# SyncE's order of key stores, context loads and first-unit loads in a four-layer Flamingo block

## The chip, the cores and the metric

The kernel runs on one core of one Trainium2 chip. The metric is device time in microseconds (us) of one execution, lower is better. Before the change three executions took 1684.19, 1691.92 and 1699.02 us; the median is 1691.92 us.

## The reference

Four layers follow one another on x (4 batches x 256 tokens x 128 features). Each is a gated cross-attention of 16 heads of 8 features over a context of 1601 tokens a batch, and then a gated feed-forward part; every layer projects its own keys and values from the same context.

```
x = x + jnp.tanh(g_xattn[0]) * _L0_xattn_ref(_layernorm(x, axis=-1), ctx_1024, ctx_1024, ctxb_2048x8, ...)
x = x + jnp.tanh(g_ffn[0]) * _L0_ffn_ref(_layernorm(x, axis=-1), L0_ffn_W_fc, ...)
x = x + jnp.tanh(g_xattn[1]) * _L1_xattn_ref(_layernorm(x, axis=-1), ctx_1024, L1_xattn_q_w, ...)
x = x + jnp.tanh(g_ffn[1]) * _L1_ffn_ref(_layernorm(x, axis=-1), L1_ffn_Wr, ...)
x = x + jnp.tanh(g_xattn[2]) * _L2_xattn_ref(_layernorm(x, axis=-1), ctx_1024, L2_xattn_wq, ...)
x = x + jnp.tanh(g_ffn[2]) * _L2_ffn_ref(_layernorm(x, axis=-1), L2_ffn_w_freq_real, ...)
x = x + jnp.tanh(g_xattn[3]) * _L3_xattn_ref(_layernorm(x, axis=-1), ctx_1024, ctx_1024, mask_1x1xSxS2_bk1, ...)
x = x + jnp.tanh(g_ffn[3]) * _L3_ffn_ref(_layernorm(x, axis=-1), L3_ffn_gate_w, ...)
```

An attention is, with h heads and `scale = Dh ** (-0.5)`:

```
scores = jnp.einsum('bhqd,bhkd->bhqk', Q, K) * scale
attn = jax.nn.softmax(scores, axis=-1)
out = jnp.einsum('bhqk,bhkd->bhqd', attn, V)
return out.transpose(0, 2, 1, 3).reshape(B, T, H * Dh) @ Wo.T
```

The second layer has two attentions, a local one (the 256 tokens against themselves) and a global one (against the context), mixed by a gate. The fourth layer masks scores by a 256 x 1601 mask.

## The kernel before

**Stages.** The context is transposed once, in the first layer, and kept in device memory as `ctxT_d` (one 128 x 1601 f32 matrix, 800 KB, a batch). In each later layer a stage that this text calls the key stage runs over the four batches: SyncE loads `ctxT_d` of a batch into one of two slots of `ctxT`; TensorE projects keys (`score_ring`, four matmul columns of 400) and values (`exp_ring`, `pv_bank`); ScalarE writes the keys' first f16 half into `k1c` (line 824), VectorE the rest into `k2c` (line 1062), each with two slots; values go to `v_all` (ScalarE, line 831, in the third and fourth layer; VectorE, line 1069, in the second). Three DMAs of 400 KB a batch store the key halves in `k_d`, in a layout by units (`k_store`, lines 503 and 505). Then comes the attention itself, over 16 units of one batch and four heads. Queries are stored in `q_d` (`q_store` on SyncE, two parts; the third part by GpSimd at line 720).

**Attention.** For a unit, pass 1 (`kp1`, `qp1`, line 1549, or 1545 with the mask) computes scores only for their row maxima, which VectorE takes (line 1132, or 1125 with the mask); pass 2 (`kp2`, `qp2`) computes them again into `exp_ring` for the exponentials on ScalarE and the products with values. `pass1` and `pass2` each load 400 KB of keys and four 12 KB pieces of queries. TensorE's program puts the whole key stage ahead of the first score: `kv(r)`, then `attention(r)`, which starts with the 16 pieces of unit 0, then `r.ahead` = 9 pieces of unit 1 (one of them a transposition of the maxima), and then merged units.

**Who waits for whom in the key stage.** Batch 2 can be projected when its context has landed in the slot that batch 0 leaves (`c_load` waits for TensorE's batch 0). ScalarE can write batch 2's keys when batch 0's three stores have landed (`k_out[0]`), batch 3's when batch 1's have (`k_out[1]`). The last piece of attention work waits for the copies of batch 3.

**SyncE's order.** SyncE carries out `k_prep` in program order, and a wait of it holds everything behind: contexts 0 and 1, the query stores, context 2, keys of batch 0, context 3, keys of batch 1, then a wait and the loads of the first units (in the second layer the eight loads of 256 KB each for the local attention, `local_loads`, lines 530 and 531), then keys of batches 2 and 3. In the second layer the loads of the first global units (`loads_start`) stand behind all stores and are followed by `local_maxima`, small loads (line 539) that the local attention's second pass (line 1652) waits for; the local first pass is line 1640.

**The mask.** In the fourth layer the mask is transposed on TensorE (`mask_turn`, line 1512, 13 times, eight matmuls each, copied by ScalarE at lines 841 to 846), one turn behind each of the first 13 pieces of unit 0.

## Time and profile before

| | |
|---|---|
| median of three executions | 1691.92 us |
| the profiled execution's own time | 1697.42 us |
| its span, first to last instruction | 1695.7 us |
| TensorE busy | 1508.3 us, 89% |
| VectorE busy | 1305.3 us, 77% |
| ScalarE busy | 1164.5 us, 69% |
| GpSimd busy | 149.2 us, 9% |
| mean granted TensorE clock | 0.915 of 2.4 GHz |
| moved by DMA | 119.39 MB, mean 70 GB/s |

Key stages stand at about 398 to 426 us (second layer), 902 to 930 us (third) and 1232 to 1260 us (fourth). A row of the timeline is: start, duration, engine, line, operation, what it writes and reads, how many, and in brackets the idle time ahead of it on its engine and what ended it. SPq rows are SyncE issuing DMAs: their duration is the issue, not the transfer. A granted clock of 1.00 is 2.4 GHz, 0.50 is 1.2 GHz.

### The profile page before, as it was taken

Reading aid. Unit: us, or ns where it says so; the run is one execution under the profiler, and the core shown is the slowest. Engines: PE = TensorE matmul, PEld = TensorE weight load, DVE = VectorE, ACT = ScalarE, POOL = GpSimd, SP = SyncE. Lnnn points to the kernel's source line nnn. Section 1 sums busy time; section 2 is a strip of 40 time slices with the busy share of each in tenths; the row PEclk is TensorE's granted clock in tenths of the full one; section 3 lists DMA queues with packets and bytes.
Section 4 is the critical chain, followed back from the end, with each engine's and each line's share of the span. In section 5 each row is a group of like instructions: output and inputs, shape, how many; then the busy total and the mean of one; then the engine's idle time right before and its main releaser. Section 6 shows DMA issues by size and latency. Waiting matters only on the chain.

```text
span 1695.7 us, 45795 instructions
## 1 busy us (share of the span) xinstructions
PE 1508.3 (89%) x15521; PEld 657.7 (39%) x15521; DVE 1305.3 (77%) x2224; ACT 1164.5 (69%) x2209; POOL 149.2 (9%) x246
## 2 busy tenths in 40 slices
PE   6789999978689999995997799999788999999977
PEld 4423333346233333334674233332453444434355
DVE  5789999546778999944875999997447888888258
ACT  3269999843357899982984499998354777777636
POOL 4200000012000000002221000000100000000012
PEclk9789999989588999996998799999787999999969
DMA  8932122105311221210116221121061111111001
GB/s 205 308 109 65 56 65 56 61 1 167 98 34 45 56 64 54 65 37 13 51 52 188 62 66 55 54 65 52 22 207 45 46 43 45 53 43 44 15 18 33
DMA packets 85286, 119.39 MB, mean 70 GB/s; under 512 B 18967, under 2 KB 57390, under 8 KB 85198
## 3 DMA queue, kind: packets, MB, share of 16 engines
q1 hardware_dynamic: 81694, 109.05, 22.1%
q0 software_dynamic: 2560, 8.20, 1.6%
q8 instruction: 59, 0.97, 0.2%
q10 hardware_dynamic: 944, 0.93, 0.2%
q14 instruction: 29, 0.24, 0.0%
HBM read 83.48 MB, written 34.49 MB: 70 GB/s over the span
## 4 chain that ended last, share of the span: by engine, by line
PE 66%; DVE 16%; issue 8%; ACT 3%; DMA 2%; SPq 2%; POOL 1%; DVEq 0%; ACTq 0%; POOLq 0%
PE pv_bank L1587 21%; DVE mx L1132 11%; PE exp_ring L1575 10%; PE score_ring L1549 5%; PE exp_ring L1567 4%; PE score_ring L1545 4%; PE score_ring L1815 4%; PE exp_ring L1826 3%; PE exp_ring L1572 3%; PE score_ring L1470 2%; PE exp_ring L1477 2%; DMA k_d<-k2c 2%; PE pv_bank L1663 1%; PE score_ring L1728 1%; ACT early L876 1%
## 5 line engine op out<-in xcount | busy, mean ns | idle before, releaser
L876 ACT ACTIVATE early<-exp_ring 128x512 f32<-128x512 f32 (+1 forms) x1664 | 884.3, 599 | 233.8 <-PE exp_ring L1575 115.6
L1132 DVE TENSOR_REDUCE mx<-score_ring 128x2 f32<-128x802 f32 (+1 forms) x768 | 703.2, 984 | 36.4 <-PE score_ring L1549 36.4
L1587 PE MATMUL pv_bank<-early,vg 128*32 128x256 f32 x6656 | 528.5, 396 | 0.7 <-issue 0.2
L1549 PE MATMUL score_ring<-kp,qp 64*128 64x401 f16 (+1 forms) x1536 | 310.8, 350 | 36.0 <-DVE mx L1132 32.0
L1575 PE MATMUL exp_ring<-qp,kp 64*128 64x512 f16 (+1 forms) x1248 | 313.6, 390 | 16.1 <-DMA qp<-ms 11.7
L1587 PEld LDWEIGHTS pv_bank<-early,vg 128*32 128x32 f32 x6656 | 139.1, 108 | 239.5 <-issue 117.1
L1575 PEld LDWEIGHTS exp_ring<-qp,kp 64*128 64x128 f16 (+1 forms) x1248 | 95.3, 95 | 194.7 <-ACT early L876 152.0
L1549 PEld LDWEIGHTS score_ring<-kp,qp 64*128 64x128 f16 x1536 | 76.2, 93 | 194.8 <-DVE mx L1132 169.1
L1545 PE MATMUL score_ring<-kp,qp 64*64 64x400 f16 (+1 forms) x1024 | 137.3, 355 | 11.3 <-DVE mx L1125 9.1
L1567 PE MATMUL exp_ring<-qp,kp 64*64 64x512 f16 x832 | 129.8, 399 | 2.8 <-DMA qp<-ms 2.8
L1572 PE MATMUL exp_ring<-ctxT,mask_eye 64*64 64x512 f16 x800 | 126.1, 385 | 0.0
L698 POOL COPY vg<-v_all 128x416 f32 (+1 forms) x48 | 25.4, 533 | 813.3 <-PE pv_bank L1587 760.6
L942 ACT ACTIVATE early<-score_ring,b_now 128x512 f32<-128x512 f32 x96 | 67.6, 704 | 23.0 <-PE score_ring L1815 22.9
L1312 DVE TENSOR_TENSOR v_all<-early,v_all 128x512 f16<-128x512 f32 x96 | 64.7, 695 | 24.1 <-ACT v_all L944 23.5
L1125 DVE CUSTOM_DVE_ANT_1 wprT<-score_ring,mask_add 128x800 f16<-128x800 f32 x64 | 63.7, 996 | 21.9 <-PE score_ring L1545 19.4
L1062 DVE SCALAR_TENSOR_TENSOR k2c<-score_ring,cols,k1c 128x401 f16<-128x401 f32 (+1 forms) x64 | 38.3, 634 | 54.6 <-ACT k1c L824 53.9
L1125 DVE CUSTOM_DVE_ANT_0 wfcT<-score_ring,mask_add 128x802 f16<-128x802 f32 x64 | 63.5, 992 | 15.9 <-PE score_ring L1545 14.5
L1125 DVE CUSTOM_DVE_ANT_0 wprT<-score_ring,mask_add 128x802 f16<-128x802 f32 x64 | 63.5, 992 | 14.6 <-PE score_ring L1545 12.4
L1182 DVE TENSOR_SCALAR rec<-score_ring 128x16 f32<-128x16 f32 x32 | 5.6, 174 | 88.6 <-PE score_ring L1728 88.6
L1826 PE MATMUL exp_ring<-v_all 128*128 128x128 f16 x1152 | 69.7, 219 | 3.0 <-DVE v_all L1312 2.8
L1567 PEld LDWEIGHTS exp_ring<-qp,kp 64*64 64x64 f16 x832 | 42.2, 105 | 77.0 <-issue 69.6
L1826 PEld LDWEIGHTS exp_ring<-v_all 128*128 128x128 f16 x1152 | 66.4, 98 | 12.4 <-issue 7.0
(271 smaller groups left out, 1504.1 us busy)
## 6 DMA issues: line engine op xcount, KB each, us to landing
kp<-k_d SPq DMA_DIRECT2D x128, 400.2 KB
k_d<-k1c SPq DMA_DIRECT2D x32, 400.2 KB, 6.9
ctxT<-ctxT_d SPq DMA_DIRECT2D x12, 800.5 KB, 5.8
qp<-q_d SPq DMA_DIRECT2D x512, 12.0 KB
k_d<-k2c SPq DMA_DIRECT2D x16, 400.2 KB, 7.9
k_d<-v_loc POOLq DMA_DIRECT2D x12, 400.2 KB, 11.1
ctxT_d<-ctxT SPq DMA_DIRECT2D x4, 800.5 KB, 7.0
o_all<-in_ctx SPq DMA_DIRECT2D x4, 768.0 KB
```

Source lines behind the costliest of these rows:

```text
L876: act.activation(pt[g][0:rows_, 2 * h:2 * h + 2, :], bank[0:rows_, :].rearrange("p (i q) -> p i q", q=S), ACT.Exp).then_inc(exped, 1)
L942: act.activation(hT[hf][:, c, :], PB[(hf * cc + c) % 4], func, bias=b1_now[k][:, c:c + 1], scale=1.0 / WSCALE)
L1125: dve.tensor_tensor_reduce(out=masked[j % 2][:, :, 0:w], in0=src, in1=mask_add[:, qt, c:c + 2, 0:w], scale=1.0, scalar=-3.0e38, op0=ALU.ad ...
L1132: dve.tensor_reduce(dst, src, AX.X, ALU.max).then_inc(score_free, 1)
L1545: ins = pe.matmul(pa[slot][u:u + 2 * R, z, 0:w], qp1[par][rows_, i, qt * P + u:qt * P + u + 2 * R], kp1[par][rows_, at:at + w], start=True ...
L1549: ins = pe.matmul(pa[slot][:, z, 0:w], qp1[par][rows_, i, qt * P:qt * P + P], kp1[par][rows_, at:at + w], start=True, stop=True)
L1567: pe.matmul(bank[out_, :], kp2[par][half, at:at + 2 * R], qp2[par][half, 2 * h:2 * h + 2, :], start=True, stop=False)
L1572: ins = pe.matmul(bank[out_, :].rearrange("p (i q) -> p i q", q=S), mask_eye[half, half], hide.unsqueeze(1).broadcast_to([2 * R, 2, S]), s ...
L1575: ins = pe.matmul(bank[0:rows_, :], kp2[par][half, s * P:s * P + rows_], qp2[par][half, 2 * h:2 * h + 2, :], start=True, stop=True)
L1587: ins = pe.matmul(po[R * j:R * j + R, 0:S], vg[par][0:rows_, s, j, :], pt[g][0:rows_, j, :], start=(s == 0), stop=(s == r.kt - 1))
L1815: ins = pe.matmul(PB[(hf * cc + c) % 4], wus[k][wp][:, c * P:c * P + P], xs[xp][:, hf * 512:hf * 512 + 512], start=(i == 0), stop=(i == 2))
L1826: ins = pe.matmul(PB[4 + hf][:, T * D:T * D + D], hs[hf][hp][:, c, T * P:T * P + P], wds[k][wp][:, c * D:c * D + D], start=(c == 0 and i = ...
```

## The change

SyncE's `k_prep` is split into one for the first layer, `k_prep_first`, with the same order as before, and one for the later layers with another order. In the third and fourth layer: keys of batch 0, context 2, the wait for the landed keys of batch 0 and the query stores, pass 1 loads of units 0 and 1, keys of batch 1, context 3, pass 2 load of unit 0, keys of batches 2 and 3. In the second layer: the waits for the query and local key stores and the eight local loads, then keys of batch 0, context 2, keys of batch 1, context 3, keys of batches 2 and 3, and then the local maxima of batch 0 ahead of the wait for all key stores. In TensorE's program the 13 mask turns of the fourth layer move from between the pieces of unit 0 to ahead of the pieces of unit 1, two a piece. `aside` is always false in the new code, so the lines under it are not built; `kv_key` and `kv_value` emit what `kv` emitted.

```
+            def k_prep(r):
+                g, l = r.ctx, r.layer
+                for i in range(2):
+                    sp.wait_ge(ctx_out[i], 16 * B // 2)
+                c_load(r, g, 0)
+                c_load(r, g, 1)
+                q_store(l)
+                if l == 1:
+                    sp.wait_ge(q_out, 16 * Q_DMAS[l])
+                    sp.wait_ge(q_out2, 16 * l * Q2_DMAS)
+                    sp.wait_ge(padded, 16 * B * (len(RUNS) - 1))
+                    sp.wait_ge(lk_out, 16 * LK_DMAS)
+                    local_loads()
+                k_store(r, g, 0)
+                c_load(r, g, 2)
+                if l > 1:
+                    sp.wait_ge(q_out, 16 * Q_DMAS[l])
+                    sp.wait_ge(q_out2, 16 * l * Q2_DMAS)
+                    sp.wait_ge(k_out[0], 48 * (B // 2 * g + 1))
+                    pass1(r, 0, 0)
+                    pass1(r, 1, 1)
+                k_store(r, g, 1)
+                c_load(r, g, 3)
+                if l > 1:
+                    sp.wait_ge(fill, r.fill0)
+                    pass2(r, 0, 0)
+                k_store(r, g, 2)
+                k_store(r, g, 3)
+                if l == 1:
+                    local_maxima([0])
...
-            def loads_start(r):
+            def loads_behind_local(r):
                 pass1(r, 0, 0)
                 pass1(r, 1, 1)
-                if r.layer == 1:
-                    local_maxima()
-                    sp.wait_ge(fill, RUNS[LOCAL].fill0 + HG * HG)
-                elif r.u0:
-                    sp.wait_ge(fill, r.fill0)
+                local_maxima(range(1, B))
+                sp.wait_ge(fill, RUNS[LOCAL].fill0 + HG * HG)
                 pass2(r, 0, 0)
...
                     for k, j in r.pieces(first=True):
                         piece(0, 0, k, first=True)
-                        if r.mask and j < KT:
-                            mask_turn(j)
                 for k in range(r.ahead):
+                    if r.mask:
+                        for m in range(2 * k, min(2 * k + 2, KT)):
+                            mask_turn(m)
                     piece(1, 1, k)
```

How the order moves on SyncE in the third layer, behind the query stores (the fourth layer reads alike). Here `ctxT<-ctxT_d` is a context load, `k_d3<-k1c` and `k_d3<-k2c` are key stores, `kp1_0`, `kp1_1` and `qp1_0`, `qp1_1` are pass 1 loads of units 0 and 1. Before:

```order
L497 DMA ctxT<-ctxT_d 128x1601 [waits v_ps,k_ps]
L503 DMA k_d3<-k1c 16x8x1601 [waits k_1]
L503 DMA k_d3<-k1c 16x8x1601
L505 DMA k_d3<-k2c 16x8x1601 [waits k_2]
L497 DMA ctxT<-ctxT_d 128x1601 [waits v_ps,k_ps]
L503 DMA k_d3<-k1c 16x8x1601 [waits k_1]
L503 DMA k_d3<-k1c 16x8x1601
L505 DMA k_d3<-k2c 16x8x1601 [waits k_2]
L515 DMA kp1_0<-k_d3 128x1601 [waits k_out_0,q_out2,q_out]
L517 DMA qp1_0<-q_d2 24x256 x4
L515 DMA kp1_1<-k_d3 128x1601
L517 DMA qp1_1<-q_d2 24x256 x4
```

And after the change:

```order
L520 DMA k_d3<-k1c 16x8x1601 [waits k_1]
L520 DMA k_d3<-k1c 16x8x1601
L522 DMA k_d3<-k2c 16x8x1601 [waits k_2]
L514 DMA ctxT<-ctxT_d 128x1601 [waits v_ps,k_ps]
L532 DMA kp1_0<-k_d3 128x1601 [waits k_out_0,q_out2,q_out]
L534 DMA qp1_0<-q_d2 24x256 x4
L532 DMA kp1_1<-k_d3 128x1601
L534 DMA qp1_1<-q_d2 24x256 x4
L520 DMA k_d3<-k1c 16x8x1601 [waits k_1]
L520 DMA k_d3<-k1c 16x8x1601
L522 DMA k_d3<-k2c 16x8x1601 [waits k_2]
L514 DMA ctxT<-ctxT_d 128x1601 [waits v_ps,k_ps]
```

Batch 0's stores now come ahead of context 2, and the wait for `k_out_0` with the four rows of pass 1 loads now stands ahead of batch 1's stores and context 3, which it stood behind.

On SyncE in the second layer, behind the query stores (`w_up`, `w_dn`, `kp2`, `wfcT` and `wprT` are the places that the local queries and keys are loaded into). Before:

```order
L497 DMA ctxT<-ctxT_d 128x1601 [waits v_ps,k_ps]
L503 DMA k_d2<-k1c 16x8x1601 [waits k_1]
L503 DMA k_d2<-k1c 16x8x1601
L505 DMA k_d2<-k2c 16x8x1601 [waits k_2]
L497 DMA ctxT<-ctxT_d 128x1601 [waits v_ps,k_ps]
L503 DMA k_d2<-k1c 16x8x1601 [waits k_1]
L503 DMA k_d2<-k1c 16x8x1601
L505 DMA k_d2<-k2c 16x8x1601 [waits k_2]
L530 DMA w_up_0<-q_d1 128x4x256 [waits lk_out,padded,zeroed,q_out2,q_out]
L531 DMA kp2_0<-k_d1 128x4x256
L530 DMA w_up_1<-q_d1 128x4x256
L531 DMA kp2_1<-k_d1 128x4x256
```

And after the change:

```order
L547 DMA w_up_0<-q_d1 128x4x256 [waits lk_out,padded,zeroed,q_out2,q_out]
L548 DMA kp2_0<-k_d1 128x4x256
L547 DMA w_up_1<-q_d1 128x4x256
L548 DMA kp2_1<-k_d1 128x4x256
L547 DMA w_dn_0<-q_d1 128x4x256
L548 DMA wfcT<-k_d1 128x4x256
L547 DMA w_dn_1<-q_d1 128x4x256
L548 DMA wprT<-k_d1 128x4x256
L520 DMA k_d2<-k1c 16x8x1601 [waits k_1]
L520 DMA k_d2<-k1c 16x8x1601
L522 DMA k_d2<-k2c 16x8x1601 [waits k_2]
L514 DMA ctxT<-ctxT_d 128x1601 [waits v_ps,k_ps]
```

The eight local loads and their wait moved from behind batch 1's stores to ahead of batch 0's, and both context loads went with the stores to behind them.

On TensorE in the fourth layer, where unit 0's scores start (`kp1_0` is unit 0, `kp1_1` unit 1, `mask01` the mask). Before, at the start of unit 0:

```order
L1545 MATMUL score_ring_0<-kp1_0,qp1_0 64x401 [waits in1_0,score_free,k_2,v_ok]
L1545 MATMUL score_ring_0<-kp1_0,qp1_0 64x401 x3
L1512 MATMUL exp_ring_0<-ident16,mask01 64x128 x8
L1545 MATMUL score_ring_1<-kp1_0,qp1_0 64x401 [waits score_free]
L1545 MATMUL score_ring_1<-kp1_0,qp1_0 64x401 x3
L1512 MATMUL exp_ring_1<-ident16,mask01 64x128 x8
L1545 MATMUL score_ring_0<-kp1_0,qp1_0 64x401 [waits score_free]
L1545 MATMUL score_ring_0<-kp1_0,qp1_0 64x401 x3
L1512 MATMUL exp_ring_2<-ident16,mask01 64x128 x8
L1545 MATMUL score_ring_1<-kp1_0,qp1_0 64x401 [waits score_free]
```

And after the change, where unit 1 starts:

```order
L1573 MATMUL score_ring_1<-kp1_0,qp1_0 64x400 [waits score_free]
L1573 MATMUL score_ring_1<-kp1_0,qp1_0 64x400 x3
L1540 MATMUL exp_ring_0<-ident16,mask01 64x128 x8
L1540 MATMUL exp_ring_1<-ident16,mask01 64x128 x8
L1573 MATMUL score_ring_0<-kp1_1,qp1_1 64x401 [waits score_free,in1_1]
L1573 MATMUL score_ring_0<-kp1_1,qp1_1 64x401 x3
L1540 MATMUL exp_ring_2<-ident16,mask01 64x128 x8
L1540 MATMUL exp_ring_0<-ident16,mask01 64x128 [waits mt_ok]
L1540 MATMUL exp_ring_0<-ident16,mask01 64x128 x7
L1573 MATMUL score_ring_1<-kp1_1,qp1_1 64x401 [waits score_free]
L1573 MATMUL score_ring_1<-kp1_1,qp1_1 64x401 x3
```

Unit 0's pieces have no turn between them any more, and unit 1's first six pieces have two each, the seventh one.

## Rows read from the trace of the kernel before

**Rows 1.** Page, part 4: chain that ended last, shares by engine.

```profile
PE 66%; DVE 16%; issue 8%; ACT 3%; DMA 2%; SPq 2%; POOL 1%; DVEq 0%; ACTq 0%; POOLq 0%
```

**Rows 2.** Stretch of third layer: busy by engine, granted clock, DMA share, GB/s.

```profile
909.00:935.00 26.00, 19.06 (x113) 13.14 (x112) 11.82 (x18) 11.38 (x24) 1.00 (x2) 0.92 0.99 307
```

**Rows 3.** Chain in order of time, end of that stage: start us, us, what.

```profile
915.96 10.04 DMA k_d<-k2c
...
928.07 1.60 ACT v_all L831 x4
```

**Rows 4.** Timeline of SyncE's DMA issues, same stage.

```profile
903.48 5.17 SPq L512 DMA_DIRECT2D q_d<-q1c  x8
...
908.75 0.53 SPq L497 DMA_DIRECT2D ctxT<-ctxT_d  x1
...
910.55 0.93 SPq L505 DMA_DIRECT2D k_d<-k2c  x1
...
914.02 1.90 SPq L503 DMA_DIRECT2D k_d<-k1c  x2
...
922.26 1.61 SPq L517 DMA_DIRECT2D qp<-q_d  x4
```

**Rows 5.** Timeline of TensorE (PE) and ScalarE (ACT), same stage and its end.

```profile
914.49 2.96 PE L1470 MATMUL score_ring<-ctxT,wsq 128*128 128x401 f32 x8 [0.92 <-DMA ctxT<-ctxT_d]
...
919.06 2.05 ACT L824 ACTIVATE k1c<-score_ring,cols 128x401 f16<-128x401 f32 x4 [4.92 <-DMA k_d<-k2c]
...
920.87 2.96 PE L1470 MATMUL score_ring<-ctxT,wsq 128*128 128x401 f32 x8 [0.52 <-DMA ctxT<-ctxT_d]
...
929.77 0.52 PE L1549 MATMUL score_ring<-kp,qp 64*128 64x401 f16 x4 [3.04 <-ACT v_all L831]
...
931.21 0.52 PE L1549 MATMUL score_ring<-kp,qp 64*128 64x401 f16 x2 [0.92 <-DVE mx L1132]
```

**Rows 6.** Landing: context loads (line 497, all), key stores (505, third layer).

```profile
DMA to landing us min/median/max: 4.4/5.8/8.3
...
DMA to landing us min/median/max: 5.5/7.3/10.0
```

**Rows 7.** Timeline of the fourth layer: SyncE, and TensorE's first score.

```profile
1238.56 0.53 SPq L497 DMA_DIRECT2D ctxT<-ctxT_d  x1
...
1259.56 0.53 PE L1545 MATMUL score_ring<-kp,qp 64*64 64x401 f16 x4 [2.10 <-ACT v_all L831]
```

**Rows 8.** Chain in the fourth layer: a turn and the next piece.

```profile
1263.44 0.58 PE exp_ring L1512 x8
...
1264.02 0.80 PE score_ring L1545 x2
```

**Rows 9.** Timeline of TensorE, same layer, two pieces without turns.

```profile
1281.61 1.80 PE L1545 MATMUL score_ring<-kp,qp 64*64 64x401 f16 x8 [0.45 <-DVE mx L1125]
```

**Rows 10.** Timeline of the second layer: GpSimd's local key stores, TensorE.

```profile
397.51 6.25 POOL L655 DMA_DIRECT2D k_d<-xn  x12
...
410.04 2.96 PE L1470 MATMUL score_ring<-ctxT,wsq 128*128 128x401 f32 x8
...
426.31 0.63 PE L1640 MATMUL score_ring<-kp,w_up 32*128 32x256 f16 x8 [3.50 <-DVE v_all L1069]
...
443.25 0.62 PE L1652 MATMUL exp_ring<-w_up,kp 32*128 32x256 f16 x6 [1.13 <-DMA w_up<-on]
```

**Rows 11.** Landing of line 655; first and last rows of eight local loads.

```profile
DMA to landing us min/median/max: 1.9/2.3/2.5
...
L530 SPq DMA_DIRECT2D w_up<-q_d x2: 653/1790/2928, 412.7 to 414.3; - x2
...
L531 SPq DMA_DIRECT2D wprT<-k_d x1: 793/793/793, 422.6 to 422.6; - x1
```

**Rows 12.** Chain: the four matmuls of line 1486, second layer, then fourth.

```profile
391.06 1.83 PE score_ring L1486 x4
...
1227.71 3.43 PE score_ring L1486 x4
```

More of the change, by code:

```diff
@@ L150 @@
 LOCAL = 1
+Q_DMAS = [12, 20, 28, 36]
+Q2_DMAS, LK_DMAS = 4, 12
 LEAD = 7
@@ new lines, in k_prep_first @@
+            def k_prep_first(r):
+                sp.wait_ge(dconst, 4)
+                constant_rows(r)
+                ctx_load(2)
+                q_store(0)
+                for b in range(B):
+                    sp.wait_ge(ctx_e, 4 * b + 4)
+                    sp.dma_start(ctxT_d[b], ctxT[:, b % 2, :]).then_inc(ctx_out[b % 2], 16)
+                    if b == 0:
+                        ctx_load(3)
+                    k_store(r, 0, b)
+                    if b == 1:
+                        sp.wait_ge(q_out, 16 * 12)
+                        sp.wait_ge(padded0, 16 * B)
+                        sp.wait_ge(dconst, 9)
+                        sp.wait_ge(prep_w, 10)
+                        sp.wait_ge(prep_v, 11)
+                        sp.wait_ge(k_out[0], 48)
+                        pass1(r, 0, 0)
+                        pass1(r, 1, 1)
+                        pass2(r, 0, 0)
@@ L531, in local_loads, with local_maxima @@
                     sp.dma_start(kl[b], k_d[LOCAL][HG * b:HG * b + HG].rearrange("n p q -> p n q")).then_inc(lin[b], 16)
-            def local_maxima():
-                for b in range(B):
+            def local_maxima(batches):
+                for b in batches:
                     sp.wait_ge(lp_free, ROWS_AT[b] + 1)
@@ L821, in k_split @@
                     for c in range(4):
[L822 removed]
+                        lo, n_ = c * w + min(c, 1), w + (c == 0)
+                        bank = PB[4 + c] if aside else PB[c]
                         act.wait_ge(k_ps, 4 * n + c + 1)
[L824 removed]
+                        act.activation(k1c[:, b % 2, lo:lo + n_], bank[:, 0:n_], ACT.Identity,
                                        bias=col(BK[r.index])).then_inc(k_1, 1)
[L827 removed]
+                        if aside:
+                            act.activation(kf[:, 4 * (b - 2) + c, 0:n_], bank[:, 0:n_], ACT.Identity,
+                                           bias=col(BK[r.index])).then_inc(k_f, 1)
+                    for c in range(4 if aside or not BV[r.index] else 0):
                         k = 4 if c < 3 else 1
@@ L1450, in normT, with kv_key, kv_value @@
                         ins.then_inc(ln_t, 1)
+            def kv_key(r, b, c, bank):
+                n, w = B * r.ctx + b, S2 // 4
+                lo = c * w + min(c, 1)
+                pe.matmul(bank[:, 0:w + (c == 0)], sq(WK[r.index]), ctxT[:, b % 2, lo:lo + w + (c == 0)],
+                          start=True, stop=True).then_inc(k_ps, 1)
+            def kv_value(r, b, c):
+                for k in range(4 * c, min(4 * c + 4, KT)):
+                    pr = P if k < FULL else TAIL
+                    ins = pe.matmul(PB[4 + c][0:pr, (k % 4) * VW:(k % 4) * VW + VW],
+                                    ctxT[:, b % 2, k * P:k * P + pr], sq(WV[r.index]), start=True, stop=True)
+                ins.then_inc(v_ps, 1)
             def kv(r):
                 g = r.ctx
-                w = S2 // 4
                 pe.wait_ge(q_f, 2 * (r.layer + 1))
```

70 lines of the change are left out of this document (16 added, 54 removed).

## The prediction

> **What bounds the kernel now.** I read the page first, for who ends the chain: TensorE has 66% of it, VectorE 16%, DMA only 2% and SyncE 2% [rows 1]. So most of the span cannot feel this change; it can act only where TensorE waits for SyncE's queue, and those places are the three key stages. The chain in order of time says what ends the third layer's stage: batch 1's last key store (10.04 us from its issue to its landing), which ScalarE waits for before it may write batch 3's keys, then the value copies [rows 3]. SyncE's timeline gives the order of issues and their lengths [rows 4], TensorE's and ScalarE's the waits: TensorE waits 0.92 and 0.52 us for contexts 2 and 3, ScalarE 4.92 us for batch 0's stores, and the first score follows batch 3's copies after 3.04 us of idling [rows 5]. It does not wait for its own keys. The stretch table shows the DMA engines full for these 26 us: share 0.99, 307 GB/s [rows 2]. The fourth layer's stage is the same picture [rows 7].
>
> TensorE's program is unchanged in this stage: all four batches are projected before the first score. Loading unit 0 earlier therefore starts nothing earlier, while what is put behind those loads (batch 1's stores, context 3) is just what the stage's end hangs on.
>
> **Third layer, step by step.** SyncE ends the query stores at 903.48 + 5.17 = 908.65 [rows 4]. Batch 0's keys were ready by then (before, their three stores were issued without a pause behind context 2), so its three stores now go first; as before they take 2.1 us (1.2 us for two, 0.93 for the third): 910.8. The last of them, issued at 909.9, lands 5.5 to 10.0 us later [rows 6]; with no context ahead of it I take 6.1, near the minimum: 916.0. Context 2 is issued behind them, 910.8 instead of 908.75, lands at about 917, and TensorE does batch 2 until about 923. That isn't on the path. SyncE stands until 916.0, then issues ten loads at 0.40 us each (four took 1.61 [rows 4]) and two gaps: 4.2 us, 920.2. Batch 1's stores take 2.1 to 3.0 us (their first two took 1.90 [rows 4]): 2.4, so 922.6, where before they were out by about 917. Then context 3, formerly issued just ahead of 914.02, lands 4.4 / 5.8 / 8.3 us later [rows 6]; behind 1.2 MB of stores I take 6.2: 928.8. Batch 1's stores land at about the same time, so one wait covers both.
>
> From there TensorE needs its whole batch: batch 2 ran from 914.49 to 920.35 (920.87 less 0.52 idle), 5.9 us [rows 5]. Copies and the first score add 0.5 (four copies took 1.60, and the last is a small one [rows 3]). Sum 935.2.
>
> To this comes the clock. TensorE would idle from about 923 to 928.8. In the trace it was at 2.4 GHz at 929.77 after 3.0 us of idling (four matmuls in 0.52 us) and at 1.2 GHz at 931.21 (two in 0.52) [rows 5]; a six-us hole should end in the low clock. At its start after such a pause a run of four matmuls took 3.43 us where it took 1.83 in the second layer [rows 12], 1.6 us more; batch 3 is longer, so I take 2.0 us. End 937.2 against 929.77: **+7.4 us**. The Trainium skill ("TensorE: Matmul & The Clock Gate", "Part 1: The HAM clock gate") speaks against this change in the same way: the array's full clock is released by sustained activity and withdrawn after idling. By that rule the holes below cost their 2 us each; without it the whole sum would be 6 us less.
>
> Bounds: all short landings and no clock loss give 915.4 + 4.0 + 2.1 + 4.4 + 5.9 + 0.5 = 932.3, +2.5. All long (917.2, then 4.8 for loads issued a sixth slower, 3.0 + 8.3 + 5.9 + 2.8 + 0.5) give 942.5, +12.7.
>
> **Fourth layer.** The same issues begin at 1238.56 instead of 908.75 [rows 4, 7], so the end is 937.2 + 329.8 = 1267.0 against 1259.56 [rows 7]: **+7.5 us**, same bounds.
>
> Mask turns: before, a piece and a turn on TensorE take 0.80 + 0.58 = 1.38 us [rows 8], at the low clock; without a turn two pieces take 1.80 + 0.45 = 2.25, or 1.12 each, set by VectorE [rows 9]. Before: 13 x 1.38 + 12 x 1.12 = 31.4. After: unit 0's 16 pieces at 1.12 = 17.9; five pieces of unit 1 with two turns at 0.80 + 1.16 = 1.96; the maxima's piece with two, 1.5; one with one, 1.38; two at 1.12: 32.8. Bundled in pairs the turns overflow VectorE's shadow by more than singly: **+1.5 us** (0 if the clock is high there, 3 at worst).
>
> **Second layer.** The local loads now wait for GpSimd's local key stores, issued until 397.51 + 6.25 = 403.8 and landed 1.9 to 2.5 us after issue [rows 10, 11]: 405.7. The eight loads were issued from 412.7 to 422.6 + 0.8, 10.7 us with two issues of about 3 us against a full queue; the shortest were 0.65 [rows 11]. They hold 2.1 MB, 6.8 us at 307 GB/s [rows 2]; I take 7.0 for the issue. Context 2 then has 2.1 + 1.2 MB ahead of it: 4.1 MB from about 407.2 on is 13.4 us, landing 421.6, where batch 2 began at 410.04 [rows 10]. Batch 2 takes 5.9 + 2.0 (TensorE idled twelve us): 429.5. Context 3 (6.1 MB, 428.1) is there by then. Batch 3 and copies: 435.9 against 426.31 [rows 10], +9.6. Given back: local maxima of batch 0 go ahead of the global loads, which removes at most the 1.13 us that line 1652 waited for them [rows 10]. **+8.5 us**; bounds +3.1 (issue in 6.0 us, batch 0's stores in 2.1, context 2 landing 4.4 us later at 418.2, two batches of 5.9, 0.5, no clock loss, 1.1 given back) and +13.5 (issues of 10.7 us again, 2.8 us of clock).
>
> **Sum.** 7.4 + 7.5 + 1.5 + 8.5 = 24.9 us. Nothing downstream absorbs it: behind each stage comes attention in which TensorE is busy. The profiled execution took 1697.4 us, 5.5 more than the median of the runs; so 1722.3 in its terms, and 1691.9 + 24.9 = **1716.8 us** against the median.
>
> **Rivals.**
> - *Cheap.* Short landings and a clock that stays up: about 19 (the sum less 6) less 5 of shorter waits, +14, 1706 us. For it: the queues are emptier when SyncE stands. Against: a hole of six us. 0.17.
> - *Dear.* The local loads block the queue as before and the landings are at their medians or above: +34, 1726 us. For it: share 0.99 [rows 2]. Against: fewer transfers overlap. 0.17.
> - *Hidden.* The bytes are the same and the DMA engines full, so each stage ends with the last byte as before: within 3 us, 1692. Against: TensorE waits for particular bytes, and SyncE standing about five us per layer leaves the engines empty. 0.04.
> - *Faster.* Batch 1's stores, whose 10.04 us end the stage [rows 3], no longer share the engines with a context issued ahead (0.8 MB, 2.6 us at 307 GB/s). If they kept their place, three stages end 2.6 us sooner and the local maxima give 1.1: 1683 us. It decides at batch 0's landing: with 4.2 us of loads between, it must land by 914.0 - 4.2 = 909.8, before its last store's issue ends. 0.04.
>
> **How the numbers follow.** The forecast, 1709 to 1725 us, has 0.58. The range 1700 to 1729 takes in the cheap rival and the dear one; its low end is the sum of all low bounds (2.5 + 2.5 + 0 + 3.1 = 8.1), its high end +37, short of all high bounds together (41.9), which need every landing at its maximum. About 1% is what a measurement can tell from no change, here 17 us. Slower by over 1% (above 1708.8): forecast, dear and 0.02 of the cheap one, 0.77. Within 1%: the rest of the cheap one and the hidden one, 0.19. Faster: 0.04.
>
> **What would show it.** In the third and fourth layer SyncE's pass 1 loads are issued at about 916 and 1246 from the old starts, batch 1's stores six us later than before; TensorE waits about 6 us for context 3 where it waited 0.5, and the chain shows that load and batch 3's matmuls at the low clock in place of the 10.04 us store. In the second, TensorE's wait of some 12 us stands ahead of batch 2. Unit 0's masked pieces come every 1.12 us and unit 1's first ones every 2. I am wrong if batch 0's stores land within 4 us, if context 3 overtakes them, or if TensorE does not wait for it.

## The result and the profile after

The changed kernel takes 1730.15 us (median of six executions, 1722.51 to 1732.12) against 1691.07 us (1684.19 to 1699.02, six): a ratio of 1.0215, 95% interval 1.0188 to 1.0242. It is slower by 39 us where 25 were forecast. Its median lies 1.2 us above the high end of the range, 1729 us; reckoned from the 1691.92 us that the prediction started from, the ratio gives 1728.3 us, just inside it. The ratios in this text leave out single executions far above the rest: one of e9 (1763.1 us), one of e11 (2023.6 us) and two of the kernel before (3206.7 and 4334.1 us).

| | before | after |
|---|---|---|
| the profiled execution's own time | 1697.42 us | 1732.12 us |
| its span | 1695.7 us | 1730.4 us |
| TensorE busy | 1508.3 us, 89% | 1525.4 us, 88% |
| VectorE busy | 1305.3 us, 77% | 1307.0 us, 76% |
| ScalarE busy | 1164.5 us, 69% | 1167.3 us, 67% |
| mean granted TensorE clock | 0.915 | 0.902 |
| moved by DMA | 119.39 MB | 119.39 MB |

The bytes and the instructions are the same; TensorE is busy 17 us longer, with a mean granted clock of 0.902 in place of 0.915. Part 4 of the page after, the chain that ended last by engine, beside [rows 1]: DMA has 3% where it had 2%, VectorE 17% where it had 16%.

```profile
PE 66%; DVE 17%; issue 8%; DMA 3%; ACT 3%; POOL 1%; SPq 1%; DVEq 0%; ACTq 0%; POOLq 0%
```

I cut both traces at the same events of TensorE: the first key matmul of a stage, the first score, the first fill (the first matmul of pass 2, whose result goes to the exponentials), the heads' output. A hole is a stretch in which TensorE waits for a context, and the masked entry is the time from the first masked score to the first masked fill. Durations in us:

| stretch | before | after | difference | forecast |
|---|---|---|---|---|
| second layer, key stage (first key matmul to first score) | 27.81 | 37.69 | +9.9 | +9.6 |
| first local score to first local fill | 16.94 | 15.82 | -1.1 | -1.1 |
| local attention (first fill to heads out) | 59.64 | 65.92 | **+6.3** | 0 |
| third layer, key stage | 27.65 | 36.83 | **+9.2** | +7.4 |
| fourth layer, key stage | 27.59 | 38.05 | **+10.5** | +7.5 |
| first masked score to first masked fill | 30.36 | 31.56 | +1.2 | +1.5 |
| everything else | | | -1.2 | 0 |

Together +34.7, the difference of the spans. The two medians differ by 4 us more; the profiled execution of before was 6 us above its median.

**Third layer.** SyncE's DMA issues in the timeline after, beside [rows 4] (start, length of the issue, engine, line):

```profile
917.83 5.16 SPq L529 DMA_DIRECT2D q_d<-q1c  x8
...
924.32 0.87 SPq L522 DMA_DIRECT2D k_d<-k2c  x1
925.29 1.12 SPq L514 DMA_DIRECT2D ctxT<-ctxT_d  x1
930.24 0.34 SPq L532 DMA_DIRECT2D kp<-k_d  x1
...
934.34 1.19 SPq L520 DMA_DIRECT2D k_d<-k1c  x2
...
936.71 1.23 SPq L514 DMA_DIRECT2D ctxT<-ctxT_d  x1
```

The stage began 14.35 us later than before (916.47 against 902.12), so the forecast's 910.8, 916.0, 920.2 and 922.6 stand for 925.2, 930.4, 934.6 and 937.0 here. The rows say 925.2 (end of the third store), 930.2 (SyncE goes on: batch 0's stores have landed), 934.3 and 936.7. What came behind is in the chain in order of time (start us, us, what):

```profile
936.71 8.36 DMA ctxT<-ctxT_d
...
945.11 4.62 PE score_ring L1477 x8
949.73 2.68 PE exp_ring L1483 x24
...
952.62 0.67 issue
```

Context 3 lands 8.4 us after its issue, not 6.2. Batch 3 and what follows take 8.2 us, where 8.4 were forecast. In place of the store of 10.04 us that ended the stage before [rows 3] there is now this load.

The stretch beside [rows 2] (26 us from 923.3: PE, PEld, DVE, ACT and POOL busy with counts, granted clock, DMA share, GB/s) shows that the DMA engines are no longer full, 0.82 and 261 GB/s in place of 0.99 and 307:

```profile
923.30:949.30 26.00, 17.28 (x74) 11.61 (x73) 6.13 (x10) 9.88 (x19) 0.00 (x0) 0.80 0.82 261
```

**Fourth layer.** The same chain; batch 3's matmuls take 5.53 us here, 0.9 more than in the third layer:

```profile
1276.14 8.42 DMA ctxT<-ctxT_d
...
1284.61 5.53 PE score_ring L1477 x8
```

And the masked pieces, TensorE's timeline beside [rows 8] and [rows 9], at the end of unit 0 and the start of unit 1:

```profile
1308.75 0.87 PE L1573 MATMUL score_ring<-kp,qp 64*64 64x400 f16 x4 [0.20 <-DVE mx L1147]
1309.91 0.87 PE L1573 MATMUL score_ring<-kp,qp 64*64 64x400 f16 x4 [0.29 <-DVE mx L1147]
1310.71 1.07 PE L1540 MATMUL exp_ring<-ident,mask 128*64 128x128 f16 x16
1311.72 0.88 PE L1573 MATMUL score_ring<-kp,qp 64*64 64x401 f16 x4
1312.53 1.07 PE L1540 MATMUL exp_ring<-ident,mask 128*64 128x128 f16 x16
```

Unit 0's pieces come 1.16 us apart here, unit 1's with two turns 1.81 us, without idling.

**Second layer.** SyncE's first and last local load and context 2, then TensorE's batch 2, first local score and first local fill, beside [rows 10] and [rows 11]:

```profile
404.70 0.40 SPq L547 DMA_DIRECT2D w_up<-q_d  x1
...
409.40 0.69 SPq L548 DMA_DIRECT2D wprT<-k_d  x1
...
412.79 1.17 SPq L514 DMA_DIRECT2D ctxT<-ctxT_d  x1
...
420.56 5.70 PE L1477 MATMUL score_ring<-ctxT,wsq 128*128 128x401 f32 x8 [11.21 <-DMA ctxT<-ctxT_d]
...
435.62 0.41 PE L1668 MATMUL score_ring<-kp,w_up 32*128 32x256 f16 x8 [0.80 <-issue]
...
451.44 0.62 PE L1680 MATMUL exp_ring<-w_up,kp 32*128 32x256 f16 x6 [0.23 <-DMA w_up<-on]
```

The eight loads took 5.4 us to issue, not 7.0, but TensorE got context 2 at 420.56, after a hole of 11.2 us. The prediction's sum by bytes, 407.2 + 13.4, is 420.6; it writes 421.6. The wait for the local maxima fell from 1.13 to 0.23 us. What the forecast didn't have is behind: the local attention after the change, as a stretch from first fill to heads out, and the same stretch before:

```profile
451.44:517.36 65.92, 56.39 (x512) 18.75 (x512) 44.48 (x48) 38.05 (x80) 4.32 (x16) 0.63 0.12 33
```

```profile
443.25:502.89 59.64, 49.70 (x512) 17.60 (x512) 43.79 (x47) 37.94 (x80) 4.32 (x16) 0.76 0.08 21
```

The same 512 matmuls take TensorE 56.4 us in place of 49.7, at a mean granted clock of 0.63 in place of 0.76: it rises to 1.00 about 46 us behind the first fill, where it did so after 27 us.

### The profile page after: what moved, and what is told of

Same layout as the page of the kernel before. It is cut to its first block, busy times and chain, and to the rows that moved or that the text cites. A ratio compares the mean times of both kernels' runs of the same rounds, so it can differ in the third digit from the quotient of the medians.

```text
span 1730.4 us, 45795 instructions
## 1 busy us (share of the span) xinstructions
PE 1525.4 (88%) x15521; PEld 664.3 (38%) x15521; DVE 1307.0 (76%) x2224; ACT 1167.3 (67%) x2209; POOL 149.2 (9%) x246
## 2 busy tenths in 40 slices
DMA packets 85286, 119.39 MB, mean 69 GB/s; under 512 B 18967, under 2 KB 57390, under 8 KB 85198
## 4 chain that ended last, share of the span: by engine, by line
PE 66%; DVE 17%; issue 8%; DMA 3%; ACT 3%; POOL 1%; SPq 1%; DVEq 0%; ACTq 0%; POOLq 0%
PE pv_bank L1615 21%; DVE mx L1154 10%; PE exp_ring L1603 9%; PE score_ring L1577 5%; PE exp_ring L1595 4%; PE score_ring L1844 4%; PE score_ring L1573 3%; PE exp_ring L1855 3%; PE exp_ring L1600 3%; PE score_ring L1477 3%; DMA ctxT<-ctxT_d 2%; PE exp_ring L1483 2%; PE pv_bank L1691 1%; DVE wfcT L1147 1%; PE score_ring L1757 1%
## 5 line engine op out<-in xcount | busy, mean ns | idle before, releaser
L1477 PE MATMUL score_ring<-ctxT,wsq 128*128 128x400 f32 (+1 forms) x128 | 59.9, 622 | 34.2 <-DMA ctxT<-ctxT_d 28.2
L964 ACT ACTIVATE early<-score_ring,b_now 128x512 f32<-128x512 f32 x96 | 67.6, 704 | 23.1 <-PE score_ring L1844 23.0
L843 ACT ACTIVATE k1c<-score_ring,cols 128x401 f16<-128x401 f32 (+1 forms) x64 | 38.2, 597 | 63.2 <-PE score_ring L1477 61.2
```

What stands on the lines that cost most here:

```text
L1477: pe.matmul(bank[:, 0:w + (c == 0)], sq(WK[r.index]), ctxT[:, b % 2, lo:lo + w + (c == 0)], start=True, stop=True).then_inc(k_ps, 1)
```

## The experiments

Times are medians; ratios are against the kernel before in the same rounds, with 95% intervals. "Stage" is the stretch from first key matmul to first score. Each duration in this table is read from one profiled execution (us):

| kernel | stage 2 | local attention | stage 3 | stage 4 | masked score to fill | ratio |
|---|---|---|---|---|---|---|
| before | 27.8 | 59.6 | 27.7 | 27.6 | 30.4 | 1 |
| after | 37.7 | 65.9 | 36.8 | 38.1 | 31.6 | 1.0215 |
| e1 mask turns only | 27.2 | 58.3 | 27.0 | 27.4 | 30.3 | 1.0003 [0.9969, 1.0038] |
| e2 second layer only | 37.6 | 65.9 | 26.8 | 27.4 | 30.4 | 1.0093 [1.0058, 1.0128] |
| e3 layers 3 and 4 only | 27.5 | 54.5 | 37.4 | 37.1 | 25.2 | 1.0118 [1.0038, 1.0199] |
| e5 layers 3, 4 and mask | 27.3 | 55.8 | 37.6 | 37.7 | 31.3 | 1.0133 [1.0081, 1.0185] |
| e4 swap only | 27.3 | 58.3 | 30.6 | 31.3 | 25.2 | 1.0033 [1.0000, 1.0066] |
| e7 swap and wait | 27.3 | 58.3 | 31.2 | 31.3 | 25.2 | 1.0028 [1.0000, 1.0056] |
| e6 holes filled | 38.2 | 59.6 | 35.0 | 37.6 | 28.9 | 1.0157 [1.0115, 1.0199] |
| e8 keys first | 27.3 | 54.5 | 27.6 | 27.0 | 30.2 | 0.9991 [0.9963, 1.0018] |
| e9 entry kept busy | 27.8 | 54.5 | 27.0 | 27.4 | 25.2 | 0.9958 [0.9931, 0.9985] |
| e10 turns put back | 38.0 | 65.9 | 36.5 | 38.0 | 24.8 | 1.0198 [1.0160, 1.0236] |
| e11 local scores kept busy | 27.8 | 61.0 | 27.2 | 27.9 | 30.9 | 1.0050 [1.0027, 1.0073] |
| e13 e8 and e9 together | 28.6 | 55.9 | 27.6 | 28.5 | 24.8 | 0.9981 [0.9951, 1.0011] |

### One part at a time: e1, e2, e3, e5

e1 is the kernel before with the last hunk of the diff shown above, nothing else.

> The kernel before with only the mask turns moved from unit 0's pieces to unit 1's, two a piece. If the turns cost what the prediction worked out, the fourth layer takes 1.5 us more between the first score and the end of unit 1's ninth piece (31 us before) and the median moves by 0 to 3 us. If the turns are the cause of part of the missing 10 us, by 5 us or more. The key stages should be as long as before (27.8, 27.7 and 27.6 us).

1693.6 us, no measurable difference, and the masked entry takes 30.3 us as before. Moving the turns is free by itself: TensorE idles 1.23 us between unit 0's first pieces and falls to the low clock all the same (two pieces of four matmuls take 0.68 us at first, and 1.86 us three us later).

e2 has the new order in the second layer only (in e2 and in the later kernels with another order `k_prep_new` is a second `k_prep`):

```
-                        k_prep(r)
+                        (k_prep_new if l == 1 else k_prep)(r)
...
+                local_loads()
+                k_store(r, g, 0)
+                c_load(r, g, 2)
+                k_store(r, g, 1)
+                c_load(r, g, 3)
+                k_store(r, g, 2)
+                k_store(r, g, 3)
+                local_maxima([0])
```

> The kernel before with the new order in the second layer alone (local loads first, local maxima of batch 0 ahead of the global loads). Theory of late transfers: the key stage from first key matmul to first local score grows by 8 to 11 us, the rest stays, so +8 to +11 us in all. Rival, the clock: the local attention behind it also runs more of its 16 units at the low clock (3.75 us a unit instead of 2.46; about 6.5 units low before, 12 in the changed kernel), so +13 to +17 us in all. If that was chance, the number of low units is as before.

1708.5 us, 16 more than before. Stage and local attention are those of the changed kernel to 0.1 us (37.6 and 65.9), so the slow local attention belongs to the order of the second layer.

e3 has the new order in layers 3 and 4 only, e5 that and the mask turns:

```
+                k_store(r, g, 0)
+                c_load(r, g, 2)
+                sp.wait_ge(k_out[0], 48 * (B // 2 * g + 1))
+                pass1(r, 0, 0)
+                pass1(r, 1, 1)
+                k_store(r, g, 1)
+                c_load(r, g, 3)
```

> The kernel before with the new order in the third and fourth layer alone. Theory of late transfers and clock: each of the two stages grows by 9 to 10 us as in the changed kernel, +18 to +21 us in all, and the second layer's local attention shows about 6.5 low units as before. If the parts hinder one another, the sum of this, the second layer's and the mask's runs is well off the whole change's +36 us.

> The kernel before with the new order in the third and fourth layer and the moved mask turns. With the new order alone the first masked fill came 25.2 us after the first masked score (30.4 us before), since TensorE entered the attention at the high clock; with the moved turns alone it came after 30.3 us. Theory that the two interact (unit 0's pieces without turns leave TensorE so idle that the clock falls, and the paired turns then run at the low clock): 31 to 32 us, as in the changed kernel, so 6 us more than the new order alone. Rival, that the turns are free: 25 us again.

e3 takes 1710.9 us and e5 1715.5. The parts add up: e2 and e5 are 15.9 and 23.1 us above before in their rounds, 39.0 in sum, and the change costs 39.1. So close a match is luck: e5 has two executions, and its interval is 9 us wide to either side. The surprise is the masked entry. e3, with the turns in their old place and the new order, has 25.2 us there, 5 less than before; e5 has 31.3. The stretches of e3 and of e5, from first masked score to first masked fill:

```profile
1271.01:1296.18 25.17, 19.90 (x203) 8.17 (x205) 22.36 (x48) 8.18 (x15) 0.97 (x2) 0.81 0.22 69
```

```profile
1274.72:1306.04 31.32, 25.50 (x202) 10.40 (x204) 22.64 (x48) 7.52 (x15) 0.97 (x2) 0.55 0.17 54
```

The same matmuls at a granted clock of 0.81 and of 0.55. So the small term of the mask (+1.2) hides two larger ones: the new order gives 5 us back here, and the moved turns, on top of that order, take 6 away.

### What in layers 3 and 4 costs the 9 us: e4, e7

e4 only puts each batch's stores ahead of the context load (K0, C2, K1, C3, then the loads as before; K is a batch's key stores, C a context load). e7 adds SyncE's wait for batch 0's stores behind C2, without any load behind it.

> The kernel before with one part of the new order in the third and fourth layer: batch 0's stores ahead of context 2 and batch 1's ahead of context 3, while the first units' loads stay behind batch 1's stores. Theory that SyncE's standing for batch 0's keys and the loads behind it are the cost: each stage stays within 2 us of before (27.7 and 27.6 us), batch 0's keys land about 3 us sooner, context 2 about 2 us later, the median moves by less than 4 us either way. Rival, that late contexts are the cost by themselves: each stage grows by 3 us or more, +6 us or more in all.

> The kernel before with batch 0's stores ahead of context 2, the wait for batch 0's landed keys ahead of batch 1's stores, but the ten first-unit loads behind context 3. It parts SyncE's standing from the loads' own issue. Swap alone made the third and fourth stage 30.6 and 31.3 us, the whole new order 37.4 and 37.1. Theory that standing and loads share the rest by their lengths (standing 4 us, ten loads 4.1 us): 33 to 35 us. Rival, that the loads' bytes and issue are all of it: 31 us. Rival, that standing is all: 37 us.

They take 1697.5 and 1695.4 us, and their stages grow by 3.0 and 3.6 us in the third layer, by 3.7 in the fourth. In e4's chain context 2 is late and batch 2 runs at the low clock; batch 3 follows without a pause:

```profile
906.53 7.99 DMA ctxT<-ctxT_d
...
914.56 4.62 PE score_ring L1492 x8
...
922.08 2.70 PE score_ring L1492 x8
```

In e7's, the last store of batch 0 lands 5.78 us after its issue and SyncE stands for it from 907.4 to 911.2. Context 3 goes out 2 us later than in e4, counted from each stage's start, and takes 8.55 us, and TensorE runs batch 3 at the high clock:

```profile
905.31 5.78 DMA k_d<-k2c
...
913.56 8.55 DMA ctxT<-ctxT_d
...
922.16 2.96 PE score_ring L1492 x8
```

e3 differs from e7 only in where the ten loads stand; its chain:

```profile
914.48 7.72 DMA ctxT<-ctxT_d
...
922.24 5.70 PE score_ring L1492 x8
```

Counted from each stage's start, context 3 lands 24.6 us in for e7 and 28.0 for e3; batch 3's eight matmuls take 2.96 and 5.70 us. That is 3.3 and 2.7 us, 6.0 of the 6.2 us between the two stages (37.4 and 31.2). The context is later because it goes out later: its own landing is not longer with the ten loads ahead of it (7.72 us) than with them behind it (8.55 us in e7). So of the 9 to 10 us the swap costs 3 to 4, the wait by itself hardly more, and the ten loads ahead of batch 1's stores the other 6, half as a late context and half as a low clock.

### The clock's share: e6

The changed kernel, with matmuls whose result is thrown away in the holes: ten ahead of batch 2 in the second layer, four and five ahead of batches 2 and 3 in layers 3 and 4.

```
+                        busy = ({2: 10} if r.layer == 1 else {2: 4, 3: 5}).get(b, 0)
+                        if busy:
+                            pe.wait_ge(k_2, 4 * (n - 1) + 1)
+                        for _ in range(busy):
+                            pe.matmul(PB[0], sq(WK[r.index]), xnT[:, 0:512], start=True, stop=True)
                         pe.wait_ge(c_ld[b % 2], 16 * ((n - B) // 2 + 1))
```

> The changed kernel with matmuls of no use added on TensorE while it waits for contexts 2 and 3 (four and five of 128 x 512 f32 in the third and fourth layer, ten ahead of context 2 in the second), which write a bank that the next keys overwrite. Theory that the low clock behind the holes costs: batch 2 and 3 then start at the high clock, the third and fourth key stage are 2 us shorter each than the changed kernel's 36.8 and 38.1 us, the second 2 to 3 us shorter than 37.7, in all -6 us or more if the local attention's clock follows. Rival, that only the transfers set the stage: within 1 us of the changed kernel's stages.

1720.7 us. The ratio, 1.0157, is lower than the change's 1.0215, about 10 us, but the intervals overlap a little, so where time was saved is read from the stretches of one profiled execution. In the third layer batches 2 and 3 both ran at the high clock and the stage lost 1.8 us; batch 3:

```profile
938.50 2.96 PE L1477 MATMUL score_ring<-ctxT,wsq 128*128 128x401 f32 x8 [1.38 <-DMA ctxT<-ctxT_d]
```

In the second and fourth layer the holes were longer than the filling (3.07 and 2.00 us stayed), batch 2 of the second and batch 3 of the fourth still ran at the low clock (5.71 and 4.37 us), and the fourth layer's stage lost 0.4 us, while the second's grew by 0.5. Most of the gain lies behind the stages: the local attention took 59.6 us in place of 65.9, the masked entry 28.9 in place of 31.6.

### Which part of the order can be kept: e8

Before, with this order in layers 3 and 4: K0, C2, query stores, C3, K1, then the loads; in the second layer K0, C2, C3, K1, the local loads, K2, K3, local maxima of batch 0. (The exchange of K0 and C2 in the second layer is in the edit; the expectation does not name it.)

> An order that follows from the runs: in the third and fourth layer batch 0's key stores go ahead of the query stores, in a time in which the DMA engines are nearly idle, the query stores behind them, contexts and batch 1's stores in the old places, first loads as before; in the second layer only the local maxima of batch 0 go ahead of the global loads. Theory that batch 1's landing ends the stage: it lands about 2 us sooner and each stage is 1 to 2 us shorter than 27.7 us, the second layer gives 1.1 us, in all -3 to -6 us. Rival, that context 3 is next to end it: within 1 us of before.

1691.6 us, no measurable difference. In the third layer context 2 is late again (7.84 us) and batch 2 slow, but the stages last 27.6 and 27.0 us as before: context 3 is there when batch 2 is done, and the first score follows TensorE's last matmul after 0.68 us, where before it waited 3.04 us for the copies [rows 5]. The wait has only moved from the end of the stage to its middle. The local maxima give 1.1 us.

```profile
902.31 7.84 DMA ctxT<-ctxT_d
...
910.20 4.60 PE score_ring L1504 x8
```

### The entry of the fourth layer: e10, e9

e10 is the changed kernel with the turns put back between unit 0's pieces (the diff's last hunk undone).

> The changed kernel with one part undone: the mask turns stand between the score pieces of unit 0 again; the order of SyncE stays the new one. Earlier runs showed that the mask part alone is free, and that the new order alone has 25.2 us between the first masked score and the first masked fill, against 31.6 with the whole change. If the two parts cost these 6 us only together (the new order lets the last stage's TensorE enter at the high clock, turns between the pieces of unit 0 keep it, and turns put off to unit 1 lose it), this run has about 25.2 us there, a granted clock near 1.00 in the pieces of unit 0, and a time 5 to 6 us under the changed kernel's (1724 to 1726, 1.018 to 1.020 of before). If the 6 us come from the queue's order in the fourth layer and not from where the turns stand, it has 31 us there and the time of the changed kernel (1730).

1728.7 us, ratio 1.0198 against the change's 1.0215: the intervals overlap, so the time alone doesn't tell. The traces do: the entry takes 24.8 us in place of 31.6. From first masked score to first masked fill, e10 and then the changed kernel:

```profile
1298.37:1323.19 24.82, 19.48 (x202) 8.07 (x204) 22.28 (x48) 8.17 (x15) 0.96 (x2) 0.84 0.22 70
```

```profile
1293.71:1325.27 31.56, 25.76 (x202) 10.40 (x204) 23.22 (x48) 7.52 (x15) 0.96 (x2) 0.55 0.17 55
```

That settles where the 6 us lie: the new order alone does not cost them (e3, e10), nor do the moved turns alone (e1). The new order of the third and fourth layers brings TensorE to the first score after a pause of 0.7 us where the old one has 2.1, and with the turns between the pieces the clock then stays high.

e9 tests that on the kernel before: two thrown-away matmuls in that pause, in layers 3 and 4, no other edit.

```
+                if r.layer > 1:
+                    pe.wait_ge(k_2, 4 * B * (g + 1) - 3)
+                    for _ in range(2):
+                        pe.matmul(PB[0], sq(WK[r.index]), xnT[:, 0:512], start=True, stop=True)
                 pe.wait_ge(k_2, 4 * B * (g + 1))
```

> The kernel before with two added matmuls of 512 columns (their result is thrown away) in layers 3 and 4, in the 2 to 3 us in which TensorE waits for the last keys ahead of the first score; nothing else changes, and SyncE's order is the old one. If it is this wait of TensorE that lets its clock fall in the fourth layer (0.50 from there on with the turns at 0.58 each), the first masked fill stands 25.2 us behind the first masked score in place of 30.4, the clock in the pieces is near 1.00, and the time is 4 to 6 us under before (about 1686, ratio 0.997). If the clock falls for the work in the pieces and not for the wait, it stays 30.4 and the time is that of before within 1 us.

1685.8 us, ratio 0.9958: 0.4% less, and the only kernel here whose interval lies wholly below 1. TensorE's timeline (the added matmuls are line 1483), and the stretch to the first masked fill in e9 and in before:

```profile
1246.94 1.88 PE L1483 MATMUL score_ring<-xnT,wsq 128*128 128x512 f32 x4
1248.75 0.53 PE L1549 MATMUL score_ring<-kp,qp 64*64 64x401 f16 x4
```

```profile
1248.75:1273.94 25.19, 20.08 (x204) 8.27 (x205) 22.39 (x48) 8.18 (x15) 0.83 (x2) 0.80 0.34 115
```

```profile
1259.56:1289.92 30.36, 25.79 (x202) 9.89 (x204) 22.84 (x48) 8.18 (x15) 0.97 (x2) 0.54 0.29 94
```

The pause of 2.10 us [rows 7] is gone, the clock stays at 2.4 GHz through the pieces with turns, and the entry takes 25.2 us in place of 30.4. The other kernels with the turns between unit 0's pieces line up with it: with no pause (e13) or one of 0.67 or 0.68 us (e3, e4, e7, e10) the entry takes 24.8 to 25.2 us; with a pause of 1.03 (e8), 1.31 (e2) or 2.38 us (e11) it takes 30.2 to 30.9:

```profile
1253.25 0.53 PE L1579 MATMUL score_ring<-kp,qp 64*64 64x401 f16 x4 [1.03 <-ACT v_all L865]
```

### The local attention: e11

Before, with one thrown-away matmul behind each of the first 15 uses of the local scores (a use is four matmuls that VectorE then takes the maxima of), in the 16.9 us in which VectorE sets the pace and TensorE is idle half the time at the low clock.

```
                     for w in range(done):
                         local_scores(w)
+                        pe.matmul(PB[7][:, 0:320], sq(WK[LOCAL]), xnT[:, 0:320], start=True, stop=True)
```

> The kernel before with one added matmul of 320 columns (thrown away) behind each use of the local scores in the stretch in which VectorE sets the pace (15 uses 1.13 us apart, TensorE 0.61 us busy of each, at the low level of its clock), so that TensorE is busy for 0.9 to 1.1 us of each 1.13. If the clock in the local attention rises late because TensorE was half idle ahead of it, it is at the high level by the first local fill: units of 2.4 us in place of 3.8 from the first on, local attention 59.6 -> 51 to 54 us, the time 5 to 8 us under before (about 1685). If the rise hangs on something else (the kind of matmul, DMA traffic at that time), the clock is 0.50 there as before, local attention stays within 58 to 62 us, and the time within 2 us of before.

1702.1 us, slower. I had mis-sized the matmul: it takes about 1.3 us at the low clock, so a use takes 1.91 us in place of 1.13, and that stretch 28.0 us in place of 16.9. The question it asked is answered nevertheless. The stretches of e11, that one and then the first 30 us of the local attention:

```profile
425.01:452.99 27.98, 27.98 (x89) 9.27 (x89) 17.52 (x15) 0.00 (x0) 0.00 (x0) 0.51 0.38 124
453.00:483.00 30.00, 26.71 (x246) 9.45 (x248) 16.99 (x16) 17.80 (x37) 1.64 (x7) 0.50 0.01 2
```

TensorE was busy without a gap for 28 us at a mean granted clock of 0.51, and the clock stayed at 0.50 for 30 us more. So idling just ahead of the local attention is not what keeps the clock low there. By the Trainium skill ("TensorE: Matmul & The Clock Gate", "Part 1: The HAM clock gate") sustained activity gives the full clock back; this run measured 28 us of it without that, and the measurement decides.

### Both gains together: e13

> The two parts that paid, together: the order of e8 (context 3 ahead of batch 1's key stores, the queries' stores put behind context 2 in layers 3 and 4, batch 0's local maxima loaded ahead of the first units' loads in layer 2) and the two added matmuls of e9 ahead of the first score of layers 3 and 4. If they add up, the stages stay at 27 to 28 us, the first local fill stands 15.8 us behind the first score in place of 16.9, the first masked fill 25.2 us behind the first masked score in place of 30.4, and the time is 1685 +- 2 us, a ratio of 0.995 to 0.996: 1 us below e9 at most, which these rounds can't tell from it. If the gain of e9 hung on the old order of SyncE, the first masked fill stands at 30 us and the time is that of e8 (0.999).

1688.8 us, ratio 0.9981: not told apart from before, nor from e9, so e9's gain in time was not seen a second time. The entry took 24.8 us and the first local fill came after 15.8, as expected, but the three stages lasted 0.6 to 1.1 us longer than e9's, 2.5 us in sum, more than the 0.7 us gained on e9 by the other two.

## Why the prediction fell short

Of the 14 us that the forecast lacks, 1.8 and 3.0 lie in the key stages of the third and fourth layers and 6.3 in the local attention, the other stretches take back 1.2 in sum, and 4 are between the medians and the two profiled executions.

**Right.** The sign, that the key stages would grow, and by which waits. In the third layer the issue of batch 0's stores, their landing, the ten loads and batch 1's stores came within 0.3 us of the steps; batch 3 at the low clock took 8.2 us (8.4). TensorE waited 3.7 us for context 3, not six, since context 2 had come 1.6 us later than reckoned and batch 2 had then run at the low clock too (5.56 us in place of 2.96), which the path doesn't feel. In the second layer the stage grew by 9.9 us (9.6), though the loads' issue took 5.4 us and not 7.0: the sum went by bytes at 307 GB/s, and the engines moved 290 GB/s in the 15.8 us from the first local load to context 2. Part of that match is luck: the prediction's own terms give context 2 at 420.6 and a growth of 8.6; it wrote 421.6, and batches 2 and 3 took 0.8 us longer than reckoned. The local maxima gave back 1.1 us. The array dropped to its low clock in the holes: a batch's eight key matmuls behind them took 4.6 to 5.7 us in place of 2.96. The Trainium skill ("TensorE: Matmul & The Clock Gate", "Part 1: The HAM clock gate") has the full clock withdrawn after idling, and these rows agree.

**Wrong, the first term: context 3's landing.** The step was "lands 4.4 / 5.8 / 8.3 us later; behind 1.2 MB of stores I take 6.2". It was 8.36 and 8.42 us, so this term was 2.2 us too small. Context 2, with only batch 0's stores ahead of it, had been put at 6.2 us too and took 7.6:

```profile
925.29 7.63 DMA ctxT<-ctxT_d
```

The bytes ahead do not explain it: the context's own 0.8 MB and the 1.2 MB of stores are 6.5 us at 307 GB/s, and the ten loads, 0.9 MB more, did not have to stand ahead of it for that: in e7 they stand behind context 3 and it took 8.55 us. The stretch of 8 us that ends with the landing shows the engines busy at a share of 0.95 and 314 GB/s, 2.5 MB:

```profile
937.00:945.00 8.00, 4.43 (x29) 3.49 (x27) 1.59 (x3) 3.15 (x6) 0.00 (x0) 0.92 0.95 314
```

In e7 they moved 306 GB/s until its context 3 landed, 2.6 MB. That is more than the context and the stores hold, so other transfers moved meanwhile, and SyncE issues the next loads 1.3 us behind context 3's issue. Which of them delay a context, those ahead or those behind, no run separates. What the ten loads cost is what the steps gave them, 4.1 us of later issue. Together with the other steps the larger landing makes the third layer 9.2 and not 7.4. In the fourth, batch 3 and what follows take 9.15 us in place of 8.4 as well, hence 10.5 and not 7.5.

**Wrong, the second term: the local attention.** The sum has no term for it; of the attention behind a stage the prediction says only that nothing in it absorbs the delay. It looked for the clock at the end of each hole and let it recover within the next batch. e2, e10 and the changed kernel, the three with the hole of 11 us, all have 65.9 us there. The nine other kernels whose second layer has no such hole and no added matmul have 54.5 to 59.6, and e6, with the hole mostly filled, 59.6. So the order of the second layer costs 6 to 11 us in a stretch that begins 16 us behind its stage. That the medians differ by more than the two spans fits this, as before's profiled execution, with 59.6, is the slowest of the nine.

**Right by cancelling: the mask.** +1.5 was forecast, from pieces that run at the low clock in both kernels, and +1.2 measured; the number is right by luck. The runs show a gain of 5 us by the order (e3) and a loss of 6 by the turns with it (e3 against e5, e10 against the change).

**The rivals.** *Hidden* falls: the bytes are the same, but the DMA share is 0.82 in place of 0.99. *Faster* falls at the point named: batch 0's stores landed at what was 915.9 in the time of before, not by 909.8. *Cheap* falls with the landing and with the clock: filling the holes gave e6 1.8 us back in the third layer's stage, where both batches then ran at the high clock. *Dear* (1726 us) was nearest in time, and half its reason is right, the landings above their medians; the local loads did not block the queue.

**Open.** What lifts the clock in the local attention. The rise came 10 to 46 us behind the first fill in kernels whose matmuls there are the same; neither TensorE's busy share just before (e11) nor the stage's length orders them. Traffic of the DMA engines does not order them either: in the first 10 us behind the first fill it is 92 GB/s in the changed kernel (65.9 us), 91 in e8 (54.5) and 2 in e9 (54.5) and in before (59.6). That the second layer's order is the cause is shown by e2 against before; that it acts by the hole is only made likely by e6's single profile, and how it acts 30 us later is not shown. Open too is what a context's landing waits for beyond the bytes ahead of it. And every duration of a stretch comes from one execution of a kernel; only the ratios rest on several.

## What to carry to other kernels

A transfer that the end of a stage hangs on is priced by its landing in a stretch as full as its own, not by the median of its kind: in the third and fourth layers of the changed kernel, e3, e5 and e7 the contexts that TensorE waited for landed 6.9 to 8.6 us behind their issue, where the median over all contexts of the kernel before was 5.8. When the order of a queue makes an engine with a variable clock wait, add the work behind the hole at the low clock, and look further down for other stretches whose clock hangs on how they are entered: here the entry of the fourth layer was worth 5 us, won by a shorter pause and lost again by moving the turns, and two useless matmuls in a pause of 2 us were the only gain measured, 0.4%, which the run that joined them with e8 did not bear out. Loads for work that the program can't start yet belong behind those of the work that it waits for.

## What was not expected of the hardware

- A pause of 2.10 us ahead of the masked pieces decided whether the next 25 us ran at a granted clock of 0.54 or 0.80 (before, e9), for the same matmuls; e8 took 30.2 us there after a pause of 1.03.
- TensorE had a mean granted clock of 0.51 over 28 us in which it was never idle (e11, local scores and matmuls of 320 columns), while batches of key matmuls brought it back to 2.4 GHz within one batch: batch 3 of e4 took 2.70 us right behind a batch 2 of 4.62.
- Holes of much the same length ended at different clocks: 2.08 us left batch 2 at the high one in e6's third layer (2.96 us), 2.00 us left batch 3 at the low one in its fourth (4.37 us), TensorE's timeline of e6:

```profile
926.97 2.96 PE L1477 MATMUL score_ring<-ctxT,wsq 128*128 128x401 f32 x8 [2.08 <-DMA ctxT<-ctxT_d]
...
1276.98 4.37 PE L1477 MATMUL score_ring<-ctxT,wsq 128*128 128x401 f32 x8 [2.00 <-DMA ctxT<-ctxT_d]
```
